# First logits of a two-layer graph attention kernel: 13 products of the projection per unit instead of 16, and VectorE's loop written out

## The reference, cut to what matters

```python
xp = (x @ W).reshape(N, H, C)               # projection, 3125 x 1024 x 1024, H=4, C=256
a_src = jnp.einsum('nhc,hc->nh', xp, att_src)
a_dst = jnp.einsum('nhc,hc->nh', xp, att_dst)
e = jax.nn.leaky_relu(a_src[src] + a_dst[dst], NEG_SLOPE)   # a logit per edge and head
m = jax.ops.segment_max(e, dst, num_segments=N)             # "scan": maximum over a node's edges
ee = jnp.exp(e - m[dst])                                    # weights
z = jax.ops.segment_sum(ee, dst, num_segments=N)
out = jax.ops.segment_sum(xp[src] * (ee / z[dst])[:, :, None], dst, num_segments=N)
```

## Time and profile before

| | |
|---|---|
| Time, median of 3 runs (lowest to highest) | 2090.77 us (2086.97 to 2091.3) |
| The profiled execution's own time, its span | 2091.52 us, 2089.8 us |
| Lookup loop, first lookup to the last product that stands in it | 99.4 to 473.9 us |
| First scan to the start of the next block | 473.9 to 524.4 us |
| Gather stage of the first layer | 524.4 to 1109 us |

### The profile page before, as it was taken

The page is one execution under the profiler, slowest core; times in us unless marked ns, Lnnn a source line. Parts: engine busy times, 40 slices in busy tenths (PEclk is TensorE's granted clock), DMA queues, the critical chain, the costliest instruction groups (busy, mean ns, idle before and its releaser), DMA issues. The chain is left out here.

```text
span 2089.8 us, 51362 instructions
## 1 busy us (share of the span) xinstructions
PE 1760.7 (84%) x12291; PEld 1136.4 (54%) x12291; DVE 1598.7 (76%) x4381; ACT 1177.3 (56%) x4251; POOL 1059.9 (51%) x1564
## 2 busy tenths in 40 slices
PE   4899999997788888888883989578888888888598
PEld 3555555543465666666662877345555555555443
DVE  6577777748566666666666999479999999999677
ACT  3200000023677777777774766148788877888766
POOL 1022222220777777777770111577777777775050
PEclk9999999998899999999997999899999999999699
DMA  8445444420899999999998998466666666664567
GB/s 333 130 107 108 108 108 108 108 63 21 308 358 359 359 357 359 357 359 355 364 353 259 326 324 265 142 177 165 162 163 163 165 160 162 168 166 109 104 216 260
DMA packets 209860, 456.51 MB, mean 218 GB/s; under 512 B 41915, under 2 KB 111288, under 8 KB 209648
## 3 DMA queue, kind: packets, MB, share of 16 engines
q0 software_dynamic: 90000, 281.90, 39.6%
q1 hardware_dynamic: 89008, 144.64, 23.0%
q10 hardware_dynamic: 30672, 27.93, 6.4%
HBM read 419.97 MB, written 47.44 MB: 224 GB/s over the span
## 5 line engine op out<-in xcount | busy, mean ns | idle before, releaser
L161 POOL DMA_INDIRECT ring<-xl_table,isrc x440 | 446.6, 1015 | 151.4 <-issue 89.9
L1270 ACT ACTIVATE wone<-onehot,w 128x64 f32<-128x64 f32 x1760 | 432.3, 334 | 147.8 <-DVE onehot L1316 141.8
L1287 PE MATMUL banks<-w_sb,wone 128*64 128x256 f32 x2368 | 317.0, 393 | 78.9 <-DMA w_sb<-xp_table,isrc 48.5
L995 PE MATMUL banks<-w_sb,acc 128*128 128x512 f32 x736 | 342.3, 604 | 0.0
L161 POOL DMA_INDIRECT w_sb<-xp_table,isrc x296 | 295.5, 998 | 90.6 <-issue 46.3
L1843 ACT ACTIVATE w<-ring,pw 128x64 f32<-128x64 f32 x1320 | 325.5, 334 | 0.0
L1312 DVE TENSOR_TENSOR acc<-banks,acc 128x512 f32 x440 | 304.3, 692 | 0.0
L1890 PE MATMUL banks<-ring,ident 128*128 128x260 f32 x880 | 256.9, 415 | 0.0
L1287 PEld LDWEIGHTS banks<-w_sb,wone 128*64 128x64 f32 x2368 | 162.3, 137 | 129.0 <-issue 43.9
L1311 DVE TENSOR_TENSOR zacc<-banks,zacc 64x9 f32 x440 | 69.6, 158 | 186.5 <-PE banks L1290 170.5
L931 ACT ACTIVATE zacc<-pidx 128x450 f32<-128x450 f32 x1 | 0.6, 578 | 361.9 <-DVE onehot_t L1081 361.9
(11 more groups left out here) (343 smaller groups left out, 2874.0 us busy)
## 6 DMA issues: line engine op xcount, KB each, us to landing
acc<-xr_table SPq DMA_DIRECT2D x440, 66.0 KB
lt_bc<-local_dst ACTq DMA_DIRECT2D x110, 128.0 KB, 3.8
w<-acc SPq DMA_DIRECT2D x100, 128.0 KB, 4.5
x_table<-y POOLq DMA_DIRECT2D x25, 512.0 KB, 7.4
acc<-x_table SPq DMA_DIRECT2D x25, 512.0 KB, 3.6
low_bc<-src_low ACTq DMA_DIRECT2D x98, 128.0 KB, 4.3
acc<-in_x SPq DMA_DIRECT2D x12, 1024.0 KB, 13.8
xp_table<-xp_st SPq DMA_DIRECT2D x24, 512.0 KB
```

The lines of the kernel that those rows point to most:

```text
L161: return self.pool.indirect_dma_start(out, None, table, bass.IndirectOffsetOnAxis(ap=idx, axis=0), bounds_check=self.bound, oob_is_err=False)
L995: last = nc.tensor.matmul(psum[:, 2 * r + i], xT_all[:, u, k, :], w_sb[:, k, i * 512:(i + 1) * 512], start=(k == 0), stop=(k == KD - 1))
L1270: last = nc.scalar.activation(wone[:, s, j, h, :], onehot[:, s, j, :], ACT.Copy, scale=w9[:, bass.ds(g * U + j, 1), h:h + 1].rearrange("p ...
L1287: nc.tensor.matmul(psum[WN * a:WN * (a + 1), j, k * C:(k + 1) * C], wone[:, s, j, h, :], slots[r][:, j, h * C:(h + 1) * C], start=True, st ...
```

## The change

The products are now one stream of 384, taken in pieces by `products(count)`. In each unit the five groups take 3, 2, 3, 2 and 3 of them (`SHARE`), 13 instead of 16. After the last group 286 are done and 98 are left; before it was 352 and 32. The 98 stand between the scan's transposes: 16, 6, 28, 4, 14, 8, 8, 8 and 6. VectorE evicts tile t two groups after its last product (`EVICT_AT`), tiles 0 to 17 within the groups and 18 to 24 between the steps of the scan. Its units are all written out, so its hardware loop is gone. ScalarE clears what is free at the start of the scan (10 slots instead of 14) and four more slots at the very end.

```diff
-            KEPT = 12
+            KEPT = 8
+            HALVES = 2 * KD
+            SHARE = (3, 2, 3, 2, 3)
+            STREAM = [sum(SHARE) * (g // GU) + sum(SHARE[:g % GU + 1]) for g in range(NG)]
+            WHOLE = STREAM[-1] // HALVES
+            EVICT_AT = {1: 0, **{min(g for g in range(NG) if STREAM[g] >= HALVES * t) + 2: t for t in range(1, WHOLE + 1)}}
...
-                    act.wait_ge(s_xp, NU)
-                    for t in [*range(KEPT), *range(KEPT + 8, NU)]:
+                    act.wait_ge(s_xp, WHOLE + 1)
+                    for t in [*range(KEPT), *range(KEPT + 8, WHOLE + 1)]:
                         clear(acc[:, t, :])
...
                     for i in range(4):
                         clear(acc[:, KEPT + i, :])
+                    act.wait_ge(s_xp, NU)
+                    for t in range(WHOLE + 1, NU):
+                        clear(acc[:, t, :])
...
+                    streamed = itertools.count()
+
+                    def products(count):
+                        for n in itertools.islice(streamed, count):
+                            u, (k, i) = 1 + n // HALVES, divmod(n % HALVES, 2)
+                            if n % HALVES == 0:
+                                wait(pe, s_xe, u - 1)
...
+                            if n % HALVES == HALVES - 1:
+                                last.then_inc(s_xp, 1)
...
-                    SLICES = ((0, 3), (3, 6), (6, 9), (9, 12), (12, 16))
-
                     def unit(u, r, static):
-                        for i, (n0, n1) in enumerate(SLICES):
+                        for i in range(GU):
...
-                            halves(u + 1, 1 - r, n0, n1)
+                            products(SHARE[i])
...
-                    products(23, 1, 0, 2)
+                    products(16)
                     pe.wait_ge(s_lg, NG)
...
-                    products(23, 1, 2, 3)
+                    products(6)
                     for b in range(NB):
                         pe.wait_ge(s_vd, b + 1)
...
-                    products(23, 1, 3, 6)
+                    products(28)
                     pe.wait_ge(scan["f1"], 1)
...
-                    products(23, 1, 6, 7)
+                    products(4)
                     pe.wait_ge(scan["c"], 1)
...
-                    products(24, 0, 0, 2)
+                    products(14)
                     weights_back(0)
-                    products(24, 0, 2, 4)
+                    products(8)
                     weights_back(1)
-                    products(24, 0, 4, 6)
+                    products(8)
                     weights_back(2)
-                    products(24, 0, 6, 8)
+                    products(8)
                     weights_back(3)
+                    products(HALVES * (NT - 1) - STREAM[-1] - 92)
...
-                            if i == 1:
-                                evict_xp(u, r, LOOP[0] if m is None else m)
-                    LOOP = [None]
-                    for u in range(2):
-                        unit(u, u, u)
-                    with dve.Fori(1, PICK_UNITS // 2) as pair:
-                        LOOP[0] = pair
-                        for r in range(2):
-                            unit(2 * pair + r, r, 2)
-                    for u in range(2 * (PICK_UNITS // 2), NU):
+                            if GU * u + i in EVICT_AT:
+                                evict_xp(EVICT_AT[GU * u + i])
+                    for u in range(NU):
                         unit(u, u % 2, u)
...
+                    evict_xp(WHOLE + 1)
...
+                    evict_xp(WHOLE + 2)
                     for b in range(NB):
                         dve.wait_ge(s_vd, b + 1)
+                        if b == 2:
+                            evict_xp(WHOLE + 3)
...
                                                  ALU.add, ALU.max).then_inc(scan["c"], 1)
+                    evict_xp(WHOLE + 4)
...
                         if b >= 2:
                             shift(b - 2, back[b - 2])
-                    evict_xp(23, 1, 11)
+                        if b == 3:
+                            evict_xp(WHOLE + 5)
+                    evict_xp(WHOLE + 6)
                     first_weights(0)
```

More of the change, by code:

```diff
@@ L22 @@
 from concourse import mybir
+import itertools
 from contextlib import ExitStack
@@ L839, in gnn_kernel @@
             cin = sb("l0_cin", [TB, 2, NB, H])
-            KEPT = 12
+            KEPT = 8
[4 more added lines that the diff above has]
+            EVICT_AT = {1: 0, **{min(g for g in range(NG) if STREAM[g] >= HALVES * t) + 2: t for t in range(1, WHOLE + 1)}}
             v, sv, fw, bw = (acc[0:TB, KEPT + 2 * i:KEPT + 2 * i + 2, :].rearrange("p t (b h e) -> p (t b) h e", b=2, h=H)
                              for i in range(4))
-            assert NB == 4 and KEPT + 8 < NU and GU * NU == NG
+            assert NB == 4 and KEPT + 8 < WHOLE and GU * NU == NG and max(EVICT_AT) < NG and len(EVICT_AT) == WHOLE + 1
             s_bias = front_sem("p1_bias")
@@ L983, in look_up_sources @@
                         last.then_inc(s_hp, 1)
[L985 to L990, removed]
+                    streamed = itertools.count()
[4 more added lines that the diff above has]
+                                wait(pe, s_xe, u - 1)
+                            if u == NT - 1:
                                 last = nc.tensor.matmul(
-                                    psum[WN * i:WN * (i + 1), 2 * r], xT_all[:, u, k, 0:WN],
+                                    psum[WN * i:WN * (i + 1), 2 * (u % 2)], xT_all[:, u, k, 0:WN],
                                     w_sb[:, k, i * 512:(i + 1) * 512], start=(k == 0), stop=(k == KD - 1))
[L994 to L1002, removed]
+                            else:
+                                last = nc.tensor.matmul(
+                                    psum[:, 2 * (u % 2) + i], xT_all[:, u, k, :],
+                                    w_sb[:, k, i * 512:(i + 1) * 512], start=(k == 0), stop=(k == KD - 1))
+                            if n % HALVES == HALVES - 1:
+                                last.then_inc(s_xp, 1)
                     for k in range(FIRST_K, KD):
@@ L1048, in _ @@
                     last.then_inc(scan["t3"], 1)
-                    products(23, 1, 7, 8)
                     def weights_back(b):
@@ L1117, in pick_sources, with evict_xp @@
                             in_=picked[:].rearrange("p j t h -> p j h t"), op=ALU.add, axis=AX.X).then_inc(s_hd, 1)
-                    def evict_xp(u, r, m):
-                        if isinstance(u, int) and u == 0:
+                    def evict_xp(u):
+                        r = u % 2
+                        if u == 0:
                             dve.wait_ge(s_bias, 16)
                         dve.wait_ge(s_xp, u + 1)
-                        wait(dve, s_xs[r], 16 * m)
+                        wait(dve, s_xs[r], 16 * (u // 2))
                         nc.vector.tensor_tensor(xp_st[:, r], psum[:, 2 * r:2 * r + 2].rearrange("p a b -> p (a b)"),
```

3 lines of the change are left out of this document (removed).

## The result

| | before | changed |
|---|---|---|
| Time, median (lowest to highest) | 2090.58 us, 4 runs (2086.97 to 2091.3) | 2077.0 us, 4 runs (2076.51 to 2077.47) |
| Ratio to before, 95% interval | | 0.9927, 0.9908 to 0.9946 |
| Profiled execution | 2091.52 us, span 2089.8 | 2077.47 us, span 2075.8 |

The changed kernel is faster by 13.6 us, 0.65%. The forecast was 2077.5 us with a range of 2074 to 2083. The ratios in this document are those on record and not quotients of the medians beside them (here 0.9935); each interval holds both.

What follows compares the result with a forecast made beforehand. TensorE was taken to bound the lookup loop, the chain through VectorE the first scan. The next block starts at 417.1 + 93.8 = 510.9 instead of 524.39, 13.5 us earlier: 2078.0, or 2077.3 from the median; forecast 2077.5, range 2074 to 2083.

Steps and rivals of the forecast that it cites:

- TensorE bounds the loop, 66 x 0.86 = 56.8 us come off it: Lookup loop: 22 units lose 3 products each at 0.86 us, 56.8 us in all, if TensorE stays the bound.
- VectorE written out is worth nothing: Lookup loop: writing out VectorE's hardware loop was taken at nothing, since VectorE has spare time.
- The scan's order, step by step: First scan: TensorE's new order summed from the loop's end as zero, block ends asked for at 46.5, last products to 88.0.
- The new wait of VectorE for tile 20: First scan: VectorE's eviction of tile 20 waits for the 34th product; 7.6 us spare before TensorE asks, so cover pays.
- The wait at weights_back(2): First scan: TensorE waits 1.0 us for first_weights(0), behind the eviction of tile 23; the cover doesn't hide it.
- The wait of 0.2 at weights_back(0): First scan: the exponentials let TensorE go on at 63.5, a wait of 0.2 us replacing the one of 7.79.
- The clears end the block: End of the scan's block: ScalarE's eight clears end at 93.6, behind SyncE at 91.1; next block starts at 93.8.
- Rival 2: End of block: SyncE at 91.1, not the clears at 93.6, ends it; 2075 us; 0.07, shared with a better gather start.
- The clock: First scan: no lowered clock in the sum, though by the skill's rule each transpose burst could lose 1.7 us.
- Everything behind shifts by the same: Blocks after the first scan: unchanged code, so all start earlier by the same 13.5 us.
- from 473.9 to 417.1: End of the lookup loop: the product stream's end comes forward from 473.9 to 417.1 us.
- The slower rival: Lookup loop: groups stay at 3.30 us however few products, VectorE's turn or its round with TensorE holding them; 2127 us; 0.03.

Runs made afterwards that it cites:

- e5: Changed kernel with one more compare of 384 columns, result unused, in VectorE's turns 2 to 97; 2435.92 us, where the kernel before takes 2454.2.
- e8: Changed kernel with three more compares of 256 columns, results unused, in VectorE's turns 2 to 97; 2464.26 us, where the kernel before takes 2467.83.
- e1: Kernel before with only VectorE's hardware loop written out, no product moved; 2089.05 us, ratio 0.9985.
- e3: Changed kernel with four clears moved into ScalarE's idle time and first_weights(0) put ahead of the eviction of tile 23; 2069.8 us, ratio 0.9905.
- e2: Changed kernel with the clears of slots 18 to 21 moved to ScalarE's idle time ahead of the first exponentials; 2075.29 us, ratio 0.9918.
- e7: Changed kernel with 66 products moved from between the scan's steps to behind its last transposes, tiles 20 to 23 evicted there; 2450.74 us, ratio 0.9992.
- e9: Changed kernel again, unedited, on a third chip; 2454.5 us, ratio to before 0.9945.
- e4: Against e3: 15 products per unit instead of 13, 54 left for the scan; 2074.76 us, ratio to the kernel before 0.9930.

## Why the prediction was right

*TensorE bounds the loop, 66 x 0.86 = 56.8 us come off it.* Right. From the first lookup at 101.5 us to the last product of the loop, 416.75 + 3 x 0.86 = 419.3, it is 317.8 us; before it was 374.5. The difference is 56.7. e5 shows that VectorE could even take a compare more, and e8 where it can't.

*VectorE written out is worth nothing.* Right for this block, by e1; of the whole time e1 leaves open a gain of up to 0.3%.

*The scan's order, step by step.* On the prediction's scale, with zero at the end of the loop (now 419.3), TensorE reached the block ends at 46.5 (forecast 46.5), the transposes back at 50.8 (50.8), weights_back(0) at 63.6 (63.5) and its last products at 85.0 (85.1). The new wait of VectorE for tile 20 cost nothing, as 7.6 us of cover said: VectorE then waited 8.14 us for the block ends. The wait at weights_back(2) was priced at 1.0 and measured at 1.25; e3 removes it and gets it back. The wait of 0.2 at weights_back(0) has no bracket in TensorE's timeline, but it is there: the 14 products ahead take 482.89 - 470.64 = 12.25 us, 0.2 more than 14 x 0.86, and the exponentials end at 482.23 + 0.61 = 482.84:

```profile
470.64 12.28 PE L1006 MATMUL banks<-w_sb,acc 128*128 128x512 f32 x28
...
482.23 0.61 ACT L951 ACTIVATE acc<-acc 110x512 f32<-110x512 f32 x1
```

*The clears end the block.* Right: forecast 93.8 us from the loop's end to the next block, measured 513.1 - 419.3 = 93.8. Rival 2, that they don't, is out. It was priced at 2.5 us, and moving the clears away in e2 gave 2.7.

*The clock.* No burst of transposes was followed by a lowered clock: the granted clock is 1.00 in the whole window. The Trainium skill ("TensorE: Matmul & The Clock Gate", Part 4: PE-mode transpose) says that a transpose doesn't count as TensorE being busy in the same way; at bursts of 1.7 us between products these traces show no effect of that. What stood ahead of a lowered clock were the waits, and both of them: the prediction gives only the stretch behind the wait of 2.76 us, and the one behind 7.79 us, at 0.50, is nearly as long. With waits of 2.76 and 3.55 us, in e7, the granted clock is 0.93 on average in the window; with none above 1.25 us it is 1.00.

*Everything behind shifts by the same.* Right for the timed medians, 13.6 us here and 13.3 in e9, not for one execution. Of the step that gave absolute times, "from 473.9 to 417.1", the end came out 2.2 us late, since the setup ahead took 2.1 us longer in this execution, and three of the four blocks behind were shorter by 0.3 to 1.9. That the profiled execution still came out 14.0 us shorter is partly luck: the 2.1 us at the front and the 2.8 us less in the blocks behind nearly cancel. Nor is it more than luck that the forecast met the median to 0.5 us, since the runs of the kernel before alone spread by 4.3. From the first barrier's release to the second the setup takes 75.2 to 77.6 us in the twelve profiles of this study, and which kernel it is makes no difference: 75.3 before and in e3, 77.6 in the changed kernel, 75.6 in the same kernel as e9.

*The slower rival*, a loop that doesn't follow, would have needed a round between VectorE and TensorE with no slack; e5 rules that out for 0.23 us more a turn. Where the whole gain goes, the prediction had too high: it asked for a turn of about 3.07 us, "eviction left out", but (14.78 + 0.7) / 5 = 3.1 is what a group may take with the evictions in it. In e8 the turn is 2.93 and the block 433.4 us, as long as before.

What the prediction did not say is that 66 is more than is needed. It treated the cover as a consequence of the number moved. e4 shows that 22 products, well placed, give most of it.

## What to carry to other kernels

When work of the bounding engine is moved from a stage that it bounds into one where it waits, the gain is the idle time that it fills there and the lowered clock that goes with those waits, not what the first stage gets shorter by; count the waits and size the pieces between them, since the total is fixed. Then look at which engine ends the stage: here four clears that were put last, though their slots were free earlier, cost 2.7 us on top of the 13.4 gained. And measure a change of this size by the length of its own stage, which repeated within 0.4 us for the same kernel, while the whole time moved by 4 and more.

## What the runs showed of the hardware

One and the same kernel took 2077 us on one chip and 2454.5 on another, 18% more. The blocks with the gathers are longer there, 728 instead of 586 us and 892 instead of 655; the block studied here is 420.0 against 420.2. On the chip of e5 to e7 the first gather stage takes 715 us. In the window from 600 to 700 us, in the first gather stage, first on the fast chip and then on the slow one:

```profile
600.00:700.00 100.00, 84.76 (x770) 60.75 (x770) 68.96 (x173) 76.12 (x312) 76.76 (x77) 1.00 0.97 354
```

```profile
600.00:700.00 100.00, 70.82 (x620) 49.57 (x619) 54.84 (x140) 60.96 (x248) 61.74 (x63) 0.97 0.86 288
```

Every engine does less in the same time, and the DMA engines move 288 instead of 354 GB/s at a busy share of 0.86 instead of 0.97. Why they do is not settled by these runs. For a comparison it means that only ratios from one chip can be set side by side, and that a gain in one stage is a smaller ratio where the others are longer: 13.4 of 2468 us is 0.54%, and e9 measured 0.55%.
